# The kernel matrix's transpose taken off TensorE: a DRAM round trip and 32x32 turns, with four projection banks

## The reference, cut to what matters

```
x: (32, 256, 512), adj: (256, 256), four weights (512, 512), two scalars
z_l = x @ W_lang.T;  z_g = x @ W_grav.T;  v = x @ W_V.T
zn  = z_l / max(|z_l|, 1e-8)
A_l = max(zn @ zn.T, 0) * not_eye
d2  = max(sq + sq.T - 2 * z_g @ z_g.T, 0),  sq = row sums of z_g * z_g
A_g = exp(-d2 / (2 sigma^2)) * not_eye
K   = w_l * rows_normalised(A_l * adj) + (1 - w_l) * rows_normalised(A_g * adj)
y   = layernorm(x + (K @ v) @ W_O.T)
```

## Time and profile before

| | |
|---|---|
| median of three runs | 719.1 us (718.97 to 719.81) |
| the profiled execution | 719.9 us |
| its span, first to last instruction | 717.8 us |
| granted clock of TensorE, mean | 0.991 of 2.4 GHz |
| TensorE busy | 97% |
| VectorE busy | 72% |
| ScalarE busy | 48% |
| POOL busy | 15% |

### The profile page before, as it was taken

One profiled execution on the slowest core, in us unless ns is written; L12 is line 12 of the kernel. 1 busy time (PEld: TensorE's weight loads), 2 busy tenths in 40 slices (PEclk: granted clock), 3 DMA queues, 4 the chain that ended last, 5 costly groups with the idle time before them and its releaser, 6 DMA issues.

```text
span 717.8 us, 10995 instructions
## 1 busy us (share of the span) xinstructions
PE 695.8 (97%) x3146; PEld 574.8 (80%) x3146; DVE 515.4 (72%) x1414; ACT 346.4 (48%) x643; POOL 110.8 (15%) x282
## 2 busy tenths in 40 slices
PE   8899999999999999999999999999999999999973
PEld 7688888888888888888888888888888888888852
DVE  4553877778777777777777777877777777876762
ACT  4333434536454544645545554644555463545445
POOL 3201001020111111020110111011110102011112
PEclk9999999999999999999999999999999999999998
DMA  9220634535453444544553444445344454353332
GB/s 286 51 60 30 154 104 118 154 112 147 148 153 115 143 136 124 153 123 125 144 141 124 128 136 152 123 128 153 125 145 126 124 153 124 96 154 96 65 86 99
DMA packets 105013, 90.75 MB, mean 126 GB/s; under 512 B 11040, under 2 KB 79136, under 8 KB 104992
## 3 DMA queue, kind: packets, MB, share of 16 engines
q1 hardware_dynamic: 104432, 88.93, 42.8%
q0 software_dynamic: 288, 1.05, 0.5%
q10 hardware_dynamic: 272, 0.52, 0.2%
HBM read 57.93 MB, written 32.54 MB: 126 GB/s over the span
## 4 chain that ended last, share of the span: by engine, by line
PE 94%; DVE 2%; ACT 1%; DMA 1%; issue 1%; POOL 0%; ACTq 0%; POOLq 0%; DVEq 0%
PE bank L951 90%; PE bank L1066 2%; PE bank L973 2%; DMA xs<-in_L_gnn_W_lang 1%; DMA out_y<-y 0%; ACT y L591 0%; DVE p_lo L679 0%; ACT m_hi L510 0%; DVE y L858 0%; ACT junk_a L583 0%; DVE m_lo L695 0%; DVE work L788 0%; DVE hT_raw L665 0%; ACT p_hi L500 0%; DVE hT_lo L673 0%
## 5 line engine op out<-in xcount | busy, mean ns | idle before, releaser
L951 PE MATMUL bank<-hT_lo,m_hi 128*128 128x512 f32 x512 | 168.0, 389 | 0.0
L543 ACT CAST p_hi<-bank 128x512 fp32r<-128x512 f32 x128 | 74.8, 584 | 127.9 <-PE bank L951 127.9
L738 DVE TENSOR_TENSOR p_lo<-bank,p_hi 128x512 fp32r<-128x512 f32 x128 | 87.7, 686 | 57.7 <-ACT p_hi L543 56.3
L951 PE MATMUL bank<-hT_hi,m_lo 128*128 128x512 f32 x320 | 124.5, 389 | 0.0
L951 PEld LDWEIGHTS bank<-hT_lo,m_hi 128*128 128x128 f32 x512 | 96.1, 188 | 20.0
L951 PE MATMUL bank<-p_hi,hT_hi 128*128 128x512 f32 x256 | 101.2, 395 | 0.0
L951 PE MATMUL bank<-wvo_hi,hT_hi 128*128 128x512 f32 x256 | 100.5, 393 | 0.0
L951 PE MATMUL bank<-wvo_lo,hT_hi 128*128 128x512 f32 x256 | 100.3, 392 | 0.0
L951 PE MATMUL bank<-wvo_hi,hT_lo 128*128 128x512 f32 x256 | 100.2, 392 | 0.0
L951 PE MATMUL bank<-p_lo,hT_hi 128*128 128x512 f32 x256 | 100.0, 390 | 0.0
L543 ACT CAST v_hi<-bank 128x512 fp32r<-128x512 f32 x64 | 37.6, 588 | 115.4 <-PE bank L951 115.4
(11 more groups left out here) (105 smaller groups left out, 1208.9 us busy)
## 6 DMA issues: line engine op xcount, KB each, us to landing
x_blk<-in_x SPq DMA_DIRECT2D x128, 128.0 KB, 3.0
x_nat<-in_x SPq DMA_DIRECT2D x32, 512.0 KB, 4.6
out_y<-y SPq DMA_DIRECT2D x32, 512.0 KB, 3.1
x_spill<-xs SPq DMA_DIRECT2D x30, 512.0 KB, 4.1
xq<-x_spill SPq DMA_DIRECT2D x120, 128.0 KB, 3.2
r_row<-r_spill SPq DMA_DIRECT2D x32, 128.0 KB, 4.2
work<-in_L_gnn_W_grav SPq DMA_DIRECT2D x2, 512.0 KB, 6.6
y<-in_L_gnn_W_O SPq DMA_DIRECT2D x2, 512.0 KB, 8.4
```

Of the source, the lines that this page charges most:

```text
L543: nc.scalar.copy(dst, src).then_inc(proj_hi, 1)
L738: nc.vector.tensor_tensor(dst, src, hi.bitcast(F32), ALU.subtract).then_inc(proj_ready, 1)
L951: last = pe.matmul(dst, lhsT, rhs, start=(n == 0), stop=(n == len(steps) - 1))
```

## The change

K.T is made the way X.T is. `spill_k` writes K (in `work`) to a DRAM tensor, `return_k` reads it back in four parts of 64 elements per run, `turn_k` turns it in 32x32 blocks on VectorE, into the buffer of the Gauss term. ScalarE and VectorE then split it from SBUF. All matrices of a batch lie in `work` with their rows' 32-element pieces side by side (`wk_row`), so the Gram sum is one instruction for both row tiles and `turn_x` two. `kt_bank` is gone; its two banks and the old `kv_bank` give a fourth projection bank and two K V banks. 1/norm is stored element by element, in order, so that it is read densely. X's transfer and the centring on VectorE stay as they were. The orders of all engines are written anew. The last pair still turns K on TensorE.

The banks, the transfers of K and the store of 1/norm:

```diff
-        proj_bank = bank[0:3]
-        kv_bank = bank[3]
+        proj_bank = bank[0:4]
         x_bank = bank[4:6]
-        kt_bank = bank[6:8]
+        kv_bank = bank[6:8]
...
+            def spill_k(q, b):
+                if not live(q):
+                    return
+                sp.wait_ge(k_ready, upto(q, 4, 2 * b + 2))
+                sp.dma_start(k_spill[b].rearrange("h p f -> p h f"),
+                             wk(b, KER).rearrange("p (h f) -> p h f", h=NT)).then_inc(k_spilled[b], 16)
+
+            def return_k(q, b):
+                if not live(q):
+                    return
+                sp.wait_ge(k_spilled[b], 16 * (q + 1))
+                run = NT * BLK
+                for j in range(P // BLK):
+                    cols = k_spill[b].rearrange("h (i c) f -> c (h i) f", c=BLK)[:, :, run * j:run * (j + 1)]
+                    sp.dma_start(wk(b, COS)[j * BLK:(j + 1) * BLK].rearrange("c (k f) -> c k f", f=run),
+                                 cols).then_inc(kq_loaded[b], 16)
+
             def store_r(p, b):
                 sp.wait_ge(pool_steps, upto(p, 6, 3 * b + 1))
-                sp.dma_start(r_spill[b], rnorm[:, b]).then_inc(r_stored[b], 16)
+                sp.dma_start(r_spill[b].rearrange("t p -> p t").unsqueeze(2), rnorm[:, b].unsqueeze(2),
+                             allow_slow_non_contiguous=True).then_inc(r_stored[b], 16)
```

SP's list for a pair:

```diff
                 q = p - 1
                 return_x(q, 1)
+                spread_r(q, 1)
+                load_blocks(p + 1, 1)
+                load_x(q, 0)
+                load_x(q, 1)
+                spill_k(q, 0)
                 load_blocks(p + 2, 0)
+                return_k(q, 0)
+                spill_k(q, 1)
                 store(q - 1, 0)
-                load_blocks(p + 1, 1)
-                spread_r(q, 1)
-                load_x(q, 0)
                 store(q - 1, 1)
-                load_x(q, 1)
+                store_r(p, 0)
                 spill_x(p, 0)
-                store_r(p, 0)
+                return_k(q, 1)
+                spread_r(p, 0)
                 return_x(p, 0)
-                spread_r(p, 0)
                 spill_x(p, 1)
                 store_r(p, 1)
 
```

VectorE's turns and the Gram sum, and its list for a pair:

```diff
                 dve.wait_ge(xq_loaded[b], BLKS * (q + 1))
                 if live(q - 1):
-                    dve.wait_ge(k_ready, upto(q - 1, 4, 2 * b + 2))
-                both = work[:, b, COS:GAUSS + 1].rearrange("p g (h k c) -> p k (g h) c", h=NT, c=BLK)
-                nc.vector.transpose(both, xq[:, b].rearrange("p (k m a) -> p k m a", m=2 * NT, a=BLK)).then_inc(xT_ready, 1)
+                    dve.wait_ge(kt_ready, upto(q - 1, 2, b + 1))
+                both = work[:, b, COS:GAUSS + 1].rearrange("p g (h i u c) -> p u i (g h) c", h=NT, u=NT, c=BLK)
+                for u in range(NT):
+                    ins = nc.vector.transpose(both[:, u], xq[:, b, u * WIDE:(u + 1) * WIDE].rearrange(
+                        "p (i m a) -> p i m a", m=2 * NT, a=BLK))
+                ins.then_inc(xT_ready, 1)
 
             def gram(q, b, g):
 
                 if not live(q):
                     return
                 dve.wait_ge(xT_ready, upto(q, 2, b + 1))
-                for t in range(NT):
-                    dst = wk_h(b, (COS, GAUSS)[g])[:, :, t].rearrange("p h (j a) -> p h j a", a=BLK)
-                    ins = nc.vector.tensor_tensor(dst, dst, x_of(b)[:, :, :, g, t], ALU.add)
-                ins.then_inc(gram_ready, 1)
-
-            def gram_of_bank(q, b, g):
+                dst = wk_k(b, (COS, GAUSS)[g])
+                own = x_of(b)[:, :, :, g].rearrange("p u j t a -> p (u j) (t a)")
+                nc.vector.tensor_tensor(dst, dst, own, ALU.add).then_inc(gram_ready, 1)
...
+            def turn_k(q, b):
+                if not live(q):
+                    return
+                dve.wait_ge(kq_loaded[b], BLKS * (q + 1))
+                dve.wait_ge(k_ready, upto(q, 4, 2 * b + 2))
+                nc.vector.transpose(wk(b, GAUSS).rearrange("p (t k c) -> p k t c", t=NT, c=BLK),
+                                    wk(b, COS).rearrange("p (k t a) -> p k t a", t=NT, a=BLK)).then_inc(kt_turned, 1)
 
...
                 q = p - 1
                 proj_lo_part(p, 0)
-                turn_x(q, 0)
+                gram(q, 0, L)
                 proj_lo_part(p, 1)
-                gram(q, 0, G)
+                cosine_masked(q, 0)
+                gauss_masked(q, 0)
+                row_factors(q, 0)
                 proj_lo_part(p, 2)
-                inverse_masked(q, 0)
                 proj_lo_part(p, 3)
-                gauss_masked(q, 0)
-                gram(q, 0, L)
-                cosine_masked(q, 0)
+                turn_x(q, 1)
+                kernel_sum(q, 0)
+                inverse_masked(q, 1)
+                gram(q, 1, G)
                 proj_lo_part(p, 4)
-                row_factors(q, 0)
                 proj_lo_part(p, 5)
-                turn_x(q, 1)
+                gram(q, 1, L)
                 proj_lo_part(p, 6)
-                gram(q, 1, G)
-                kernel_sum(q, 0)
+                cosine_masked(q, 1)
                 proj_lo_part(p, 7)
                 gauss_masked(q, 1)
-                inverse_masked(q, 1)
-                gram(q, 1, L)
+                row_factors(q, 1)
+                turn_lo(p + 1, 1 - parity, 0)
+                kernel_sum(q, 1)
+                diagonal(p, 0)
+                turn_k(q, 0)
+                turn(p + 1, 1)
                 kt_lo_part(q, 0)
-                cosine_masked(q, 1)
-                row_factors(q, 1)
-                diagonal(p, 0)
-                kernel_sum(q, 1)
+                diagonal(p, 1)
+                if is_last(p):
+                    return
+                turn_lo(p + 1, 1 - parity, 1)
+                turn(p + 2, 0)
                 residual(q, 0, 0)
-                turn_lo(p + 1, 1 - parity, 0)
-                diagonal(p, 1)
-                kt_lo_part(q, 1)
                 residual(q, 0, 1)
                 proj_lo_part(p, 8)
-                if is_last(p):
-                    return
-                turn(p + 1, 1)
+                turn_k(q, 1)
+                proj_lo_part(p, 9)
+                kt_lo_part(q, 1)
+                inverse_masked(p, 0)
                 residual(q, 1, 0)
-                proj_lo_part(p, 9)
-                turn_lo(p + 1, 1 - parity, 1)
+                turn_x(p, 0)
+                gram(p, 0, G)
+                proj_lo_part(p, 10)
+                proj_lo_part(p, 11)
                 residual(q, 1, 1)
-                proj_lo_part(p, 10)
-                turn(p + 2, 0)
-                proj_lo_part(p, 11)
```

ScalarE's list for a pair, and the one after the loop:

```diff
                 proj_hi_part(p, 0)
                 proj_hi_part(p, 1)
+                squares(q - 1, 0)
                 proj_hi_part(p, 2)
-                normalise(q - 1, 0)
                 proj_hi_part(p, 3)
-                gauss(q, 0)
+                proj_hi_part(p, 4)
+                gauss_scaled(q, 0)
                 squares(q - 1, 1)
-                proj_hi_part(p, 4)
                 proj_hi_part(p, 5)
-                gauss_scaled(q, 0)
                 proj_hi_part(p, 6)
                 proj_hi_part(p, 7)
                 gauss(q, 1)
+                normalise(q - 1, 0)
+                gauss_scaled(q, 1)
+                save_x(p, 0, 0)
+                save_x(p, 0, 1)
                 normalise(q - 1, 1)
                 kt_hi_part(q, 0)
-                turn_hi(p + 1, 1 - parity, 0)
-                save_x(p, 0, 0)
-                save_x(p, 0, 1)
-                gauss_scaled(q, 1)
                 save_x(p, 1, 0)
                 save_x(p, 1, 1)
-                kt_hi_part(q, 1)
+                if is_last(p):
+                    return
+                turn_hi(p + 1, 1 - parity, 1)
                 proj_hi_part(p, 8)
                 proj_hi_part(p, 9)
-                if is_last(p):
-                    return
-                squares(q, 0)
-                turn_hi(p + 1, 1 - parity, 1)
+                kt_hi_part(q, 1)
                 proj_hi_part(p, 10)
                 proj_hi_part(p, 11)
-
+                turn_hi(p + 2, parity, 0)
+                gauss(p, 0)
...
+            proj_hi_part(p, 9)
+            gauss_scaled(p, 0)
+            kt_hi_part(q, 1)
+            gauss(p, 1)
             squares(q, 0)
-            gauss_scaled(p, 0)
+            kt_hi_part(p, 0)
             proj_hi_part(p, 10)
-            gauss(p, 1)
-            kt_hi_part(p, 0)
             normalise(q, 0)
+            gauss_scaled(p, 1)
             proj_hi_part(p, 11)
-            gauss_scaled(p, 1)
+            kt_hi_part(p, 1)
             squares(q, 1)
-            kt_hi_part(p, 1)
             normalise(q, 1)
-            squares(p, 0)
-            normalise(p, 0)
-            squares(p, 1)
-            normalise(p, 1)
+            for b in range(2):
+                squares(p, b)
+                normalise(p, b)
 
 
         @block.vector
```

(36 more changed lines are left out.)

222 lines of the change are left out of this document (122 added, 100 removed).

## The result

The changed kernel takes 804.8 us (median of four runs, 801.96 to 809.7) against 719.2 for the kernel before on the same chip: ratio 1.120, 95% interval [1.114, 1.125]. The forecast was 707.1, from 702.5 to 713.0. The change makes the kernel 12% slower, and the prediction had given 0.10 to slower at all.

The account below looks back on a forecast made before the run. TensorE's own queue was taken as the bound. K turns removed before the last x tile -13.9, K V moved behind it -1.4, preparation -1.7, tail +5.0: -12.0 us from 719.1 gives 707.1, range 702.5 to 713.

Parts of the forecast that it names:

- r: 1/norm's store to DRAM in the loop, 256 pieces of 4 bytes: landing taken as 5.5 us, return_x behind it with margin 3.
- The walk: One loop pair followed through all queues in the new order: nothing stalls, 39.9 us per pair.
- Rival 2: Loop, slower: r's 4-byte store holds SP, return_x and turn_x, so TensorE waits for v_lo; 733 at 11 us landing; chance 0.08.
- the tail: From the last x tile's end to the span's end: 45.3 us against 40.3, +5.0, bounds +3.2 and +6.5.
- The range's lower end: Whole kernel: 702.5 us, given as preparation -3, tail +3.2 and no more.
- The chances as listed: Whole kernel: likeliest case 0.65, the others 0.20, 0.08, 0.04 and 0.03; stated as faster 0.87, same 0.03, slower 0.10.
- the four margins of the walk: Loop pair: four slacks of 0.8 to 1.6 us, walked with rounded durations, expected to keep TensorE from waiting.
- Rival 1: Small waits in the loop: tight margins overdrawn, the seam by 0.3 costing 4.5 us; 709.5 to 716; chance 0.20.
- the seam's step: Between pairs: margin 0.8 before TensorE's third projection; with three banks a stall of half a microsecond per pair.
- Rows of 32 elements: VectorE in the loop: 32-element rows in place of 128 priced at nothing; a tenth more would be 0.3 us a pair.
- The preparation's first product: Weight preparation on four banks: the first product starts at about 28.4 instead of 30.13, -1.7 us (0.5 to 3).
- The page's rule: DMA transfers under 512 B cost a read-modify-write; noted as speaking against r's store and K's 256-byte returns, size unknown.

Follow-up runs that it names:

- paired kernel: The changed kernel with 1/norm stored as before, in 128 pieces of 8 bytes, the mask product in two instructions: 710.45 us, 0.988 against the kernel before.

## Why the prediction was wrong

**The step that failed** is the one on **r**: "The nearest row is the old one, 5.5 us in the median; for a bulk store 4.1. I take 5.5." It measured 9.4, and the size is only half of the fault. The step priced the landing for the store's own readers ("Behind it on SP wait spread_r and return_x") and found a margin of 3. It left out what SP issues right behind the store without waiting for it: X's store and K's return. These were late whichever queue had issued the store; the run from POOL's queue shows that. The walk gave K of batch 1 slack in two places ("returned 31; turn_k 33.5, kt_lo 35.5, needed at 37.2"): 2.5 us before its turn and 1.7 behind kt_lo. The paired kernel shows what there was:

```profile
349.26 0.70 DVE L901 STREAM_TRANSPOSE work<-work 128x512 f32<-128x512 f32 x1
...
350.64 0.69 DVE L914 TENSOR_TENSOR kt_lo<-work,kt_hi 128x512 fp32r<-128x512 f32 x1
```

```profile
353.21 0.39 PE L1024 MATMUL bank<-v_hi,kt_hi 128*128 128x512 f32 x1
```

K is in at 348.9, 6.2 us after the first issue of its return: 0.3 before the turn, and kt_lo is done 1.9 before it is needed. In the changed kernel the same return takes 12.4. The 6.2 us more, less these 2.2, leave about 4.0 of the 4.4 that TensorE waits. So the walk also had K some 2 us too early, which alone cost nothing.

**The price of a stall.** Rival 2 counted "each microsecond more costs 15". In the loop it costs more, because TensorE runs on at 0.50 of the clock for some 13 matmuls: 4.4 us of wait became 7.1. Over the run, 93 us were lost between the preparation and the last x tile (its gram turns are at 755.84, and at 662.77 in the paired kernel, both after a wait of 1.14). Of these 52.4 are waits for kt_lo, from the row of 59.6 less the tail's 7.2, and 5.3 are the wait for v_lo at the first seam (6.8, against 1.5). The rest, some 35 us, is TensorE busy for longer, which goes with the lower clock: 666.8 against 631.3 us from 28.69 to those turns.

**Rival 2** had the cause and its place, and I gave it 0.08. Its waiter was wrong in the changed kernel (turn_x; it was turn_k, but for the first seam) and right once K's return went first. Its sum at a landing of 9.4 would have been 709 and was off by 96, because it let the landing shift one chain, and not X's store and K's return behind it. The same section said "The trace has no such store" and then took the row of a store with half the pieces. A range that takes in the bounds of an unknown cost would have needed an upper end for it, and the text gave none above 5.5. The range's lower end does not follow from its own terms either: preparation -3 and tail +3.2 give 704.0, not 702.5. The chances as listed add up to 0.88 for faster and 0.11 for slower, not 0.87 and 0.10.

**What held,** read in the paired kernel, which differs from the changed one in that store and the extra mask instruction only: 710.45 against 707.1, inside the range.
- A steady pair is 39.9 us with no wait for TensorE, VectorE at 32.10, and the four margins of the walk all held. Rival 1 did not happen.
- The fourth bank carries the gain, as the seam's step had it; its size was off: 0.92 us a pair without it, where half a microsecond was forecast.
- Rows of 32 elements cost nothing extra: the mask product (L855) takes 0.685 us in the mean, 0.684 before, and the two masked sums and the kernel sum are as close. The preparation's first product starts at 28.69 in the changed kernel, forecast 28.4.
- The tail, from the end of the last x tile to the end of the span, is 46.3 us, forecast 45.3. Its waits are in their places: 1.14 for xs (forecast 1.2), 1.74 for kt_lo(14,1) (forecast 3), 3.30 for v_lo, and 6.8 for the store of y. The five microseconds given away here were ScalarE's order; the run that changes it is 5.7 us faster.
- Of the distance of 3.3 us the profiled execution shows 2.1 in its span (707.9, forecast 705.8): 1.0 in the tail and 1.1 before it, where TensorE waits 1.5 us at the first seam. The rest is how the profiled executions lie to the medians of their kernels.

**The page's rule.** The Trainium skill, "DMA: Bandwidth & Descriptors", Specifications, says that transfers under 512 B do a read-modify-write, and the prediction noted that it speaks against this store. The runs do not bear out the size as the reason: pieces of 4 bytes 8 or 512 bytes apart are as far under 512 B as the touching ones and cost 0 to 4 us in place of 90. Whether a read-modify-write is part of what the touching ones cost, no run here shows.

## What to carry to other kernels

When a store changes from few bytes in long pieces to elements, its cost can be not its own landing but what the transfers behind it lose; list what is issued next on any queue, and ask which of them is due within some ten microseconds (here landings of 9.4 to 12.5). If elements must be stored one by one, a layout in which a partition's values follow each other, with a gap between any two, was cheap here (710.8 to 714.8), and so was turning them on VectorE first (eight pieces of 128 bytes: 708.6 against 804.8). And a stall of TensorE of some 4 us cost 1.6 times its length here, because the granted clock was 0.50 after it.

## What the runs showed of the hardware that I had not expected

- After a store of 256 pieces of 4 bytes that touch, 1 KB in all, the DMA engines move only 4 to 34 GB/s for some 7 us, and what is issued behind it lands late, from another queue too. Pieces of 4 bytes with gaps of 4 bytes land in 5.5 us, and X's store behind them in 5.7.
- Pieces of 8 bytes that touch (5.5 us, and 5.3 when there are twice as many) do not do it. No run says why those of 4 bytes do. That two neighbours share something which is written as a whole, and wait for each other, fits all sixteen runs, but is only argued; the order of the pieces, their starts and their number in a short stretch fit them as well.
- One store of 128 partitions and four of 32 behave alike without touching pieces (714.8 and 716.1), and not with them (801.0 and 826.7); this, too, stays open.
